# Head attention: the value products of a key tile made whole in every step, with new PSUM bank tables and waits for each head

## The reference

```python
q = (src @ Wq).reshape(Bb, Tt, H, DH).transpose(0, 2, 1, 3)          # H = 16 heads of DH = 16
k = (src @ Wk_c @ Wk).reshape(Bb, Tt, H, DH).transpose(0, 2, 1, 3)
v = (src @ Wv_c @ Wv).reshape(Bb, Tt, H, DH).transpose(0, 2, 1, 3)
...
q = _apply_rope(q, sin, cos)
k = _apply_rope(k, sin, cos)
attn = jnp.einsum('bhqd,bhkd->bhqk', q, k) / np.sqrt(DH).astype(np.float32)
attn = jax.nn.softmax(attn, axis=-1)
sa = jnp.einsum('bhqk,bhkd->bhqd', attn, v)
...
```

## Time and profile before

| | |
|---|---|
| median of 3 runs | 1502.27 us (1500.78 to 1505.69) |
| the profiled execution | 1504.91 us, of which the span from the first to the last instruction is 1503.2 us |
| mean granted TensorE clock | 0.958 of full speed |
| PE, DVE, ACT, POOL busy | 1374.3, 1124.6, 854.8, 379.7 us |
| maxima of the items (L1793) | 512, 617.8 us |
| exponentials (L1762) | 1024, 551.2 us |
| value products (L1709) | 3728 matmuls, 319.1 us |
| score pairs (L1688), items (L1669) | 1024 matmuls each, 254.9 and 222.8 us |

### The profile page before, as it was taken

How to read it: one execution, slowest core, us unless ns; L and a number is a source line. 1 busy time by engine, 2 the same in 40 slices (tenths; PEclk the granted TensorE clock), 3 DMA queues, 4 the chain that set the end, 5 groups by cost and what they waited for, 6 DMA issues and landing times. The chain is left out here.

```text
span 1503.2 us, 26898 instructions
## 1 busy us (share of the span) xinstructions
PE 1374.3 (91%) x9725; PEld 811.4 (54%) x9725; DVE 1124.6 (75%) x1803; ACT 854.8 (57%) x1573; POOL 379.7 (25%) x384
## 2 busy tenths in 40 slices
PE   6999895946999999999999999989999999879995
PEld 3655574722333333333333333335888888778884
DVE  3786572639999999999999999934666766546664
ACT  2445441400888888888888888885343344223331
POOL 0343267453513000000000000101222332335553
PEclk9999997965999999999999999999999999999998
DMA  5799755554254434423334434213666553355551
GB/s 183 269 321 341 265 181 203 109 99 95 65 93 107 65 58 65 65 52 55 52 45 65 65 64 65 74 51 49 162 138 173 171 159 100 103 188 174 172 181 53
DMA packets 116321, 187.68 MB, mean 125 GB/s; under 512 B 26645, under 2 KB 65961, under 8 KB 116197
## 3 DMA queue, kind: packets, MB, share of 16 engines
q1 hardware_dynamic: 90117, 124.55, 33.6%
q0 software_dynamic: 15616, 47.81, 11.1%
q10 hardware_dynamic: 10464, 13.64, 3.0%
HBM read 104.99 MB, written 81.88 MB: 124 GB/s over the span
## 5 line engine op out<-in xcount | busy, mean ns | idle before, releaser
L1793 DVE TENSOR_REDUCE i_saT<-h_banks 128x2 f32<-128x1024 f32 x512 | 617.8, 1221 | 34.5 <-PE h_banks L1669 26.8
L1762 ACT ACTIVATE h_p<-h_banks 128x512 f32<-128x512 f32 x1024 | 551.2, 598 | 152.8 <-PE h_banks L1688 137.5
L1709 PE MATMUL h_po<-h_p,h_v 128*32 128x256 f32 (+1 forms) x3728 | 319.1, 414 | 3.5 <-ACT h_p L1762 1.4
L1688 PE MATMUL h_banks<-h_q,h_k 50*128 50x512 f32 x1024 | 254.9, 496 | 11.6 <-ACT h_p L1762 6.0
L1669 PE MATMUL h_banks<-h_k,h_q 48*128 48x512 f32 x1024 | 222.8, 431 | 32.8 <-PEq L70 18.2
L1688 PEld LDWEIGHTS h_banks<-h_q,h_k 50*128 50x128 f32 x1024 | 95.9, 184 | 236.0 <-ACT h_p L1762 191.2
L1709 PEld LDWEIGHTS h_po<-h_p,h_v 128*32 128x32 f32 x3728 | 73.4, 108 | 170.9 <-issue 84.1
L2055 PE MATMUL f_ob<-w_experts,f_h 128*128 x1032 | 134.7, 286 | 11.9 <-issue 9.8
L2055 PEld LDWEIGHTS f_ob<-w_experts,f_h 128*128 128x128 f32 x1032 | 126.0, 191 | 21.1 <-issue 21.1
L1669 PEld LDWEIGHTS h_banks<-h_k,h_q 48*128 48x128 f32 x1024 | 101.1, 194 | 58.2 <-DVE i_saT L1793 33.6
L1565 POOL COPY h_v<-h_values 128x512 f32<-128x512 f32 x14 | 8.6, 614 | 463.1 <-DMA h_values<-vh_d 463.1
(11 more groups left out here) (262 smaller groups left out, 1673.2 us busy)
## 6 DMA issues: line engine op xcount, KB each, us to landing
h_q<-q_d SPq DMA_DIRECT2D x84, 128.0 KB, 5.9
h_k<-k_d SPq DMA_DIRECT2D x84, 128.0 KB, 6.9
ot_d<-h_o ACTq DMA_DIRECT2D x32, 256.0 KB, 2.4
q_d<-t_parts SPq DMA_DIRECT2D x12, 512.0 KB, 5.0
k_d<-t_parts SPq DMA_DIRECT2D x12, 512.0 KB, 5.2
rows_d<-h_place SPq DMA_DIRECT2D x4, 1056.0 KB, 4.4
rows_d<-f_rows SPq DMA_DIRECT2D x4, 1056.0 KB, 6.2
p_xin<-in_L_attn_x SPq DMA_DIRECT2D x8, 512.0 KB, 5.1
```

What stands on the lines that cost most here:

```text
L1688: ins = nc.tensor.matmul(bank_of(key, g), k6[r][at, p, j * P:(j + 1) * P], q6[r][at, p, c * CH:(c + 1) * CH], start=True, stop=True)
L1709: ins = nc.tensor.matmul(po[h * VW:(h + 1) * VW, at], vh[n % RING][:, j, h, :], probs[u % PR][:, h, at], start=j == 0 and (part == 0 or la ...
L1762: nc.scalar.activation(probs[u % PR][:, h, :], bank_of(("PAIR", f // SIDES), f % SIDES), ACT.Exp, scale=DH ** -0.5).then_inc(exp_done, 1)
L1793: nc.vector.tensor_reduce(halfmax[n % 2][:, m, :], both_banks(("SLOT", slot)), AX.X, ALU.max)\
```

## The change

The mix is whole in every unit, behind both score pairs and both items. The two halves' order is gone, and with it the case for the last step. The bank tables have four entries instead of seven, so they repeat every two units. The transposed maxima take the first bank of the next score pair, as before, by the new table. Each matmul of a score pair waits for its own bank, and `scored` counts heads, so that an exponential waits for its own head. `Banks.before` keeps one holder for each bank in place of a list of all.

```diff
@@ -988,13 +988,13 @@
 
     def give(self, key, *banks):
         self.places[key] = banks
-        self.before[key] = [self.holder[b] for b in banks if b in self.holder]
+        self.before[key] = [self.holder.get(b) for b in banks]
         for i, b in enumerate(banks):
             self.holder[b] = (*key, i)
 
-    def before_it(self, key, kind):
-
-        return [(n, i) for was, n, i in self.before[key] if was == kind]
+    def before_it(self, key, kind, at):
+
+        return [who[1:] for who in self.before[key][at] if who and who[0] == kind]
 
 
 class Room:
@@ -1513,18 +1513,19 @@
 
         LAST = STEPS - 1
 
-        PAIR_BANKS = ((0, 1), (4, 0), (1, 2), (5, 6), (2, 3), (6, 0), (3, 4))
-        SLOT_BANKS = ((2, 3), (5, 6), (3, 4), (0, 1), (4, 5), (1, 2), (5, 6))
+        PAIR_BANKS = ((0, 2), (3, 4), (5, 4), (0, 1))
+        SLOT_BANKS = ((5, 6), (0, 1), (2, 3), (5, 6))
+        ROUND = len(PAIR_BANKS)
         given = Banks()
         for slot in range(turn_slot(0) + LEAD * PER - HELD + 1):
-            given.give(("SLOT", slot), *(SLOT_BANKS[3 + slot % 2] if slot != turn_slot(0) else (6,)))
+            given.give(("SLOT", slot), *(SLOT_BANKS[2 + slot % 2] if slot != turn_slot(0) else (0,)))
         for h in range(LAST * UNITS * PARTS):
-            given.give(("PAIR", h), *PAIR_BANKS[h % BANKS])
+            given.give(("PAIR", h), *PAIR_BANKS[h % ROUND])
             n, m = divmod(h + ITEMS + LEAD * PER, ITEMS)
             if m == HELD and n <= STEPS:
-                given.give(("SLOT", turn_slot(n - 1)), PAIR_BANKS[(h + 1) % BANKS][0])
+                given.give(("SLOT", turn_slot(n - 1)), PAIR_BANKS[(h + 1) % ROUND][0])
             if n < STEPS:
-                given.give(("SLOT", item_slot(n, m)), *SLOT_BANKS[h % BANKS])
+                given.give(("SLOT", item_slot(n, m)), *SLOT_BANKS[h % ROUND])
         given.give(("FIRST", 0), *OF_FIRST)
         for h in range(LAST * UNITS * PARTS, STEPS * UNITS * PARTS):
             given.give(("PAIR", h), *(b % OF_FIRST.start for b in (h * SIDES, h * SIDES + 1)))
@@ -1650,8 +1651,8 @@
 
             @block.tensor
             def _(pe):
-                def emptied(key):
-                    pairs, slots = given.before_it(key, "PAIR"), given.before_it(key, "SLOT")
+                def emptied(key, at=slice(None)):
+                    pairs, slots = given.before_it(key, "PAIR", at), given.before_it(key, "SLOT", at)
                     if pairs:
                         pe.wait_ge(exp_done, max(h * SIDES + g + 1 for h, g in pairs))
                     if slots:
@@ -1682,18 +1683,18 @@
                     r, key = n % RING, ("PAIR", (n * UNITS + w) * PARTS + p)
                     if w == 0 and p == 0:
                         pe.wait_ge(shifted[r], shifts_of(n))
-                    emptied(key)
                     for g in range(SIDES):
+                        emptied(key, slice(g, g + 1))
                         at = slice(g * SIDE_AT, g * SIDE_AT + ROWS)
                         ins = nc.tensor.matmul(bank_of(key, g), k6[r][at, p, j * P:(j + 1) * P],
                                                q6[r][at, p, c * CH:(c + 1) * CH], start=True, stop=True)
-                    ins.then_inc(scored, 1)
+                        ins.then_inc(scored, 1)
 
                 def mix(n, w, part):
 
 
                     c, j = divmod(w, QT)
-                    u, last = n * UNITS + w, j == QT - 1 or n == LAST
+                    u, last = n * UNITS + w, True
                     if part == 0:
                         if j == 0:
                             pe.wait_ge(out_taken, n * NQ + c)
@@ -1744,9 +1745,7 @@
                             turn_maxima(coming[0] - 1)
                         if coming[0] < STEPS:
                             item(*coming)
-                        if u and n < LAST:
-                            mix(*divmod(u - 1, UNITS), part)
-                    if n >= LAST:
+                    if u:
                         for part in range(PARTS):
                             mix(*divmod(u - 1, UNITS), part)
                     if n == LAST:
@@ -1758,7 +1757,7 @@
                     u, h = divmod(f, GH)
                     if h == 0 and u >= PR:
                         act.wait_ge(pv_done, u - PR + 1)
-                    act.wait_ge(scored, f // SIDES + 1)
+                    act.wait_ge(scored, f + 1)
                     nc.scalar.activation(probs[u % PR][:, h, :], bank_of(("PAIR", f // SIDES), f % SIDES), ACT.Exp,
                                          scale=DH ** -0.5).then_inc(exp_done, 1)
```

## The result

The changed kernel takes 1550.91 us (median of 4 runs, 1549.44 to 1553.9), the kernel before 1501.62: ratio **1.0325** (95% interval 1.0301 to 1.035), 49 us slower. The profiled execution took 1553.9 us, 49.0 more than that of before.

The account below looks back on a forecast made before the run. PE was taken to bound the quiet stretch. 118 rounds of 5.24 us plus 14 transposed maxima of 1.05 give 633.0 against 602.2 before, 30.8 more: median 1533 us, range 1514 to 1552.

Parts of the forecast that it names:

- The hole before a: DVE idle before the even tile's first item: about 0.5 us, ended by PE, every 5.2 us.
- Other banks leave slack: Even tile's second item takes its first score pair's first bank, said to be free some 0.2 us earlier.
- 118 rounds: Two-tile rounds of the 472 items behind the prologue's 40, each taken as 5.24 us.
- The transposed maxima: Once a step they take bank 0 from the item just before; 1.05 us of DVE each, 0.95 to 1.2.
- the tiles that were to change by at most 1: Four tiles without items, where ACT sets the pace: 0, at most 1 us either way.
- the hold of a by d: Even tile's first item waits for DVE on the odd tile's second, same banks; DVE's loop 5.20 to 5.29 us.
- rival of a freed PE: No hold between those items, two tiles bound by PE's 4.66 us: 39 us faster, 1464; chance 0.05.
- Theory B: From the experiments: a whole-mix tile wants eight banks of seven, so the last instruction before the mix awaits its first exponential.
- Chunk ends: After each 8 tiles, where the mix was whole already: their cost of 0.4 to 0.7 us a chunk goes.
- Edits at nothing: Waits and signals for each head, and other small edits, cost nothing; at most 1 us in tiles without items.
- The clock rival: PE idles some 0.6 of 5.2 us, so the granted clock might fall from 1.00; chance under 0.02.
- Rotation of banks: Matmul groups should rotate through PSUM banks: kept, two tiles take PE's 4.66 us; broken, 5.24.

Follow-up runs that it names:

- the sixth experiment: The changed kernel with half of the first head's exponential of each tile left out: 1534.3 us.
- The seventh experiment: The changed kernel with each DVE maximum over half of the columns from the third step on: 1538.05 us.
- the fourth: The changed kernel with other four-entry bank tables, where no item takes a bank of the item before it: ratio 1.027 to the kernel before.
- the ninth experiment: The changed kernel with the transposed maxima in bank 6 instead of bank 0: ratio 1.0218 to the kernel before.
- Experiments 1: The kernel before with only the order changed (mix whole in every unit), old tables and pair waits: ratio 1.0303.
- the tenth experiment: The changed kernel with the order score pair, item, item, score pair, mix, and tables for it: ratio 1.0197 to the kernel before.
- the eleventh: The changed kernel with items of one head and one bank from the third step on, half of the maxima left out, banks going round: 1429.67 us.
- the fifth: The kernel of the fourth with half of the first head's exponential of each tile left out: 1502.29 us.
- the eighth experiment: The kernel before with half mixes at the chunk ends too, whole mixes only in the last step: ratio 0.9991.
- third experiment: The kernel before with only the waits and signals for each head, old order and tables: ratio 1.0014.

## Why the prediction was right, and where its sum fell short

**Right**, and in part by luck: slower, inside the range, by waits that bank tables put between PE, ACT and DVE, with PE's saving of 0.30 for two tiles unused. The hole before a is where it was put (0.59 us, ended by PE), and its loop has the size that was worked out: 5.21 in the sixth experiment against 5.20. But it isn't the loop that sets the round. In the changed kernel each tile takes 1.24 us from its start to its second item, which waits for the tile's own first exponential, then 0.43 and 1.00: 2.67, so 5.34 for two. The seventh experiment, where DVE holds no item back, has the same 2.67. Each loop alone costs most of the loss: of 2.94 us a step, 2.03 stay in the sixth experiment, which shortens the exponential, and 2.52 in the fourth, which has no hold. They lie so near each other that a sum made from the shorter one came out inside the range.

**The step that failed** is "Other banks leave slack: b takes A's first bank, free some 0.2 us earlier". It isn't free: b starts at 603.14, 0.05 behind that exponential. Nor is the bank of d, C's first, which the prediction doesn't name: d starts 0.05 behind C's first exponential. Two sizes made it look so. The first exponential of a tile starts 0.10 after its pair (601.90 + 0.49 to 602.49), not 0.04. The trace of before has both values: the 0.04 of the earlier trace rows belongs to a tile's third exponential, at 605.87, and the first, for the pair at 606.55, starts 0.10 after it:

```profile
607.15 1.09 ACT L1762 ACTIVATE h_p<-h_banks 128x512 f32<-128x512 f32 x2 [0.20 <-PE h_banks L1688]
```

In the code only the first exponential has a second thing to wait for (the mix two units before); that this makes the difference isn't shown. And a starts 0.53 behind A, not the 0.7 or so that 0.2 us of slack implies, so b comes sooner. The wait and the reload behind it bring c 0.14 us late, the round 5.36 instead of 5.24. The chunks without transposed maxima say the same: 21.38 / 4 = 5.35.

**The terms.** 118 rounds by 0.11 more are 12 to 13 us of the 18 that were missing (30.8 forecast, 49 measured). The transposed maxima cost 43.77 - 8 x 5.35 = 0.97 to 1.0 where 1.05 was set; in the ninth experiment 0.3 of it is left. Near 3 us more came in the tiles that were to change by at most 1: from the last copy of the transposed maxima to the last copy out of the sums 54.1 us instead of 51.3, with the clock as told below. In the ninth experiment, whose clock doesn't fall there, it is 51.2. Of the rest, 2.6 lie behind the head attention and 1.1 ahead of it, where nothing changed; the part behind differs by as much among the profiles of the experiments (466.7 to 472.7 us). Two readings were off and change nothing: (7.51 - 1.22) / 5 is 1.26 and not 1.25, and holds a gap of 0.13 us before the second maximum, behind which they come every 1.23 like PE's turns; and the trace has two places like the earlier trace rows, the other at 737.57.

**The cause was too narrow.** The prediction blamed the hold of a by d, and its rival of a freed PE said "Two tiles take PE's 4.66, were a not held by d". Experiments 1, 4, 7 and 10 take that hold away in four ways and keep 2.67 to 2.71 a tile by their chunks. So the rival was wrong in its condition: other tables were not enough, and it took a tile that wants fewer banks (the eleventh). The sixth shows the hold by itself: with the exponential's wait shortened it keeps the step at 42.86, where the fifth, without it, has 40.47. Theory B stands by experiments 1, 4, 5, 7, 10 and 11; that seven banks are the reason for the wait was shown by wanting fewer, not by having more.

**Chunk ends**: no stall is left there, as forecast; the halves in the eighth experiment show that there was little to gain at them. **Edits at nothing**: right for the waits and signals of each head (third experiment). **The clock rival**: not in the loop, whose granted clock is 1.00 above.

**Rotation of banks.** The hold between d and a is real (sixth experiment), but tables that rotate past it don't free PE: the fourth experiment's do and has 2.66. So what the prediction took from the Trainium skill, Perfetto Trace Analysis, section Optimizing Tensor Performance (groups rotating through different PSUM banks) tells the direction of a broken rotation here, and not the time of a kept one.

## What to carry to other kernels

Before making one step of a software pipeline longer, count the buffers that the steps in front of it now want at once; where that is one more than there are, the last of them waits for the first reader, whatever the table says. Follow that wait through to the start of the next turn as one loop, with the start-up of each engine taken from rows of the same instruction of the turn: here the tile's first exponential, not its third. A hole on the engine that looks starved names the last wait, not the loop: take it away and see whether the turn gets shorter.

## What the hardware showed unexpectedly

The granted clock fell to 0.50, the lower of its two levels, in the changed kernel's four tiles without items, after holes of 0.56 and 0.68 us on PE, far shorter than the 3.01 us of the earlier trace rows. The windows, and a mix of 1.93 us in PE's timeline there:

```profile
1020.00:1027.00 7.00, 6.35 (x41) 1.94 (x39) 4.41 (x5) 5.70 (x13) 0.00 (x0) 1.00 0.00 1
1027.00:1030.00 3.00, 2.32 (x15) 0.85 (x14) 1.76 (x4) 1.61 (x3) 0.00 (x0) 0.86 0.03 6
1030.00:1036.00 6.00, 6.00 (x28) 1.41 (x24) 0.00 (x0) 4.13 (x8) 0.00 (x0) 0.50 0.27 84
```

```profile
1027.79 0.51 PE L1689 MATMUL h_banks<-h_q,h_k 50*128 50x512 f32 x2 [0.68 <-DVE h_mparts L1812]
...
1030.37 1.93 PE L1710 MATMUL h_po<-h_p,h_v 128*32 128x512 f32 x8
```

The fourth experiment has the lower level at the same place for some 3 us (mixes of 1.49 and 1.71), the ninth and tenth not at all, so it is no fixed part of the change's cost; whether the timed runs have it can't be read from them. Nor do the holes decide it: the seventh has the same 0.56 and 0.68 us there and keeps 1.00. What did is open.

An item that waits directly before the mix starts 0.42 to 0.44 us ahead of it, instead of 0.32 to 0.34. Its weight load starts with it (603.14), where that of an item that doesn't wait starts 0.23 ahead (604.68 for c at 604.91). Before a score pair the late load costs nothing: a waits too, and B follows 0.34 behind. This 0.1 us is in the tiles of 2.65 to 2.68 us above, in the tenth experiment by a score pair in the item's place.
